# First attention: the rows of maxima go from SBUF to SBUF in three transfers, ahead of the large loads of terms

## The chip, the cores and the metric

The kernel runs on one core of one Trainium2 chip. The metric is the device time of one execution in microseconds (us); lower is better. The core's engines are TensorE (PE in the rows; its weight loads are PEld), VectorE (DVE), ScalarE (ACT), GpSimd (POOL) and SyncE (SP), which here only issues transfers. Each runs its own list of instructions in order and waits on semaphores for the others.

## The reference, cut to what matters

Two transformer layers run one after the other on 16 sequences of 256 tokens with 128 channels. The first half of the first layer, which alone is touched, is:

```python
h = _layernorm(x, axis=-1) * (1 + ca) + sa
# _L0_attn_ref, 16 heads of 8 channels
q = apply_rope(q) * scale
k = apply_rope(k)
dots = jnp.einsum('bnih,bnjh->bnij', q, k)
dots = jnp.where(mask, jnp.float32(-100000.0), dots)
attn = jax.nn.softmax(dots, axis=-1)
o = jnp.einsum('bnij,bnjh->bnih', attn, v)
return o @ Wo.T + bo
x = x + ga * _L0_attn_ref(h, ...)
```

A mixture of experts, a sparse second attention and a second mixture of experts follow.

## The kernel before

The function `attention0` handles one sequence (one batch, index k from 0 to 15) in each turn of a software pipeline. A turn mixes stages that belong to different batches: in the turn of batch k, stage C computes the scores, exponentials and outputs of batch k, D finishes the output projection of batch k-1, M and N compute the row maxima of batches k+1 and k+2 (M the second half of the groups of heads, N the first), S loads the terms of k+2, A projects, rotates and splits batch k+4, and L takes the layer norm's statistics of batch k+5. I call the turn of batch k turn k; turns -5 to -1 only fill the pipeline. The order inside a turn is written out by hand for each engine, in the `run(...)` lists at the end of each engine's block.

The scores are computed twice. Queries and keys are split into bf16 parts whose products add up to an fp32 product; the combinations ("terms", 48 rows) are written to DRAM (`a0_terms_d`) and read back into `qs` and `ks`. Each batch's terms are read back twice, 384 KB for each of `qs` and `ks` each time: by `spread_parts` into rows 64 to 111 for stages M and N (L381), and by `spread_again` into rows 0 to 47 for stage C (L394). Stages M and N compute the masked scores, and VectorE reduces each bank to the negated row maxima (`maxima`, L734). These are split into three bf16 parts, turned by TensorE (`turn_max`, L587), copied to `nparts` (48 partitions by 256) by ScalarE (`take_max`, L496), and moved into rows 48 to 50 of `qs` by `spread_max`, through DRAM (L401, then L403). Rows 48 to 50 meet ones in `ks`, so that stage C's matmul (L541) gives score minus maximum.

TensorE starts a turn with three groups of scores, which I call (0,0), (0,1) and (0,2) after the stage C part of each; every group begins with a mask matmul of stage M (L508; the one of (0,2) is the first in a turn with 512 columns). The waits that matter at a turn's start are in `open_c`: the semaphores `c_spread` (the loads of L394) and `nspread` (the row transfer of L403). Group (0,2) reuses the bank of (0,0), so it waits until VectorE has reduced that bank. After (0,2) come `outputs(3)` of the batch before (L601, L603), which waits for GpSimd's `keep(3)` (L442). Late in the turn stand the projections of stage A (L624), VectorE's rotation (L711, L713), GpSimd's sum (L422) and then the square root of the layer norm (L414, L416), and last on VectorE's list `normalise` (L700).

SP's list in a turn is `spread_again`, `spread_max`, `spread_parts`:

```python
run(sp, [("S", spread_again), ("M", spread_max), ("A", spread_parts)])
```

Of the kernel before, what the change touches and what calls it, by code (L numbers as in the profile page):

```python
# [11 lines left out]
BF16 = mybir.dt.bfloat16  # L12
# [3 lines left out]
B, L, D = 16, 256, 128  # L16
# [3 lines left out]
H, HD = 16, 8  # L20
# [228 lines left out]
def hold(eng, sem, per, b, n):  # L249


    if per * b.k + n > 0:
        eng.wait_ge(sem, b.x * per + n)


def pipeline(eng, first, last, start, end, body, turns=3):


    passes = (end - start) // turns
    for k in range(first, start):  # L260
        body(Batch(k, k))
    with eng.Fori(0, passes) as i:
        for r in range(turns):
            body(Batch(i * turns + (start + r), start + r))
    for k in range(start + passes * turns, last):
        body(Batch(k, k))


def attention0(nc, s, t, ps):
# [21 lines left out]
    TOP = ROWS  # L291
    UN = 12
    with ExitStack() as ctx:
        def sb(name, shape, dt=F32):
            return ctx.enter_context(nc.sbuf_tensor("a0_" + name, shape, dt))

        def sem(name):
            return ctx.enter_context(nc.semaphore("a0_" + name))
# [12 lines left out]
        qs = sb("qs", [M_ROW + ROWS, 3, H, L], BF16)  # L311
# [3 lines left out]
        nparts = sb("nparts", [3 * H, L], BF16)  # L315
# [5 lines left out]
        yo = sb("yo", [P, L])  # L321
        unit, pause = sb("unit", [P, 1]), sb("pause", [P, 1])
        terms_d = nc.dram_tensor("a0_terms_d", [3, 2, len(TERMS), P, L], BF16).ap()
        nparts_d = nc.dram_tensor("a0_nparts_d", [3 * H, L], BF16).ap()

        cleared = sem("cleared")
        stats_done, rstd_done, y_done = sem("stats_done"), sem("rstd_done"), sem("y_done")
# [3 lines left out]
        m_spread, c_spread = sem("m_spread"), sem("c_spread")  # L331
        m_full, m_read = sem("m_full"), sem("m_read")
        nT_full, nT_read = sem("nT_full"), sem("nT_read")
        nsplit, nstored, nspread = sem("nsplit"), sem("nstored"), sem("nspread")
        c_full, exp_done = sem("c_full"), sem("exp_done")
        kept = sem("kept")
        pv_done, o_read = sem("pv_done"), sem("o_read")
# [11 lines left out]
        def run(eng, order):  # L349

            ahead = {"D": -1, "C": 0, "M": 1, "N": 2, "S": 2, "A": 4, "L": 5}

            def body(b):
                for stage, step in order:
                    if stage == "B":
                        step(b)
                        continue
                    c = b + ahead[stage]
                    if 0 <= c.k < B:
                        step(c)  # L360
            pipeline(eng, -5, B + 1, 2, B - 5, body)

        @block.sync
        def _(sp):
            def own_rows(side, b):

                return terms_d[b.k % 3, side].rearrange("t (d h) n -> (t d) (h n)", h=H)

            def spread_parts(b):


                sp.wait_ge(split, b.x + 1)
                for n, m in RUNS:
                    sp.dma_start(terms_d[b.k % 3, 0, n:n + m].rearrange("t p n -> p t n"),
                                 parts[:, 0, TERMS[n][0]].unsqueeze(1).to_broadcast([P, m, L])).then_inc(q_stored, 16)
                for n, m in RUNS:
                    sp.dma_start(terms_d[b.k % 3, 1, n:n + m].rearrange("t p n -> p t n"), parts[:, 1, 0:m]
                                 ).then_inc(k_stored, 16)
                for dst, side, done in ((qs, 0, q_stored), (ks, 1, k_stored)):
                    sp.wait_ge(done, b.x * STORE + STORE)  # L380
                    sp.dma_start(dst[M_ROW:M_ROW + ROWS, b.k % 3].rearrange("p h n -> p (h n)"), own_rows(side, b)  # L381
                                 ).then_inc(m_spread, 16)
                if b.k == 1:
                    for name, src in (("wg", "e0_wg"), ("wu", "e0_wu"), ("wd", "e0_wd"), ("wr", "e0_wr")):
                        sp.dma_start(s["e0_w"][name][:], t[src]).then_inc(s["e0_in"], 16)
                    sp.dma_start(s["e0_w"]["bias"][:], t["L0_ffn_e_score_bias"].partition_broadcast(P)
                                 ).then_inc(s["e0_in"], 16)

            def spread_again(b):


                hold(sp, c_full, UN, b + -3, UN)
                for dst, side in ((qs, 0), (ks, 1)):
                    sp.dma_start(dst[0:ROWS, b.k % 3].rearrange("p h n -> p (h n)"), own_rows(side, b)  # L394
                                 ).then_inc(c_spread, 16)

            def spread_max(b):


                sp.wait_ge(nT_read, b.x + 1)  # L400
                sp.dma_start(nparts_d, nparts[:]).then_inc(nstored, 16)  # L401
                sp.wait_ge(nstored, b.x * 16 + 16)
                sp.dma_start(qs[TOP:TOP + 3, b.k % 3], nparts_d.rearrange("(t h) n -> t h n", h=H)).then_inc(nspread, 16)  # L403

            run(sp, [("S", spread_again), ("M", spread_max), ("A", spread_parts)])

        @block.gpsimd
        def _(pool):
# [48 lines left out]
        @block.scalar  # L457
        def _(act):
            def modulate(b):
                hold(act, a_full, A_STEPS, b, 1)  # L460
                nc.scalar.activation(hT[:, b.k % 3], ps[:, 6, 0:L], ACT.Identity, bias=sa[:], scale=ca[:]).then_inc(a_read, 1)

            def exps(g, n):
                def step(b):
                    if n == 0:
                        hold(act, pv_done, HG, b, g - 1)
                    act.wait_ge(c_full, b.x * UN + 3 * g + n + 1)
                    bank = 2 + (3 * g + n) % 2
                    if n < 2:
                        dst, src = pr[:, g % 2, 2 * n:2 * n + 2, 0:L], ps[:, bank].rearrange("p (j n) -> p j n", j=2)  # L470
                    else:
                        dst, src = pr[:, g % 2, :, L:L + P], ps[:, bank].rearrange("p (j n) -> p j n", j=HJ)
                    nc.scalar.activation(dst, src, ACT.Exp).then_inc(exp_done, 1)  # L473
                return step

            def outputs(a):
                def step(b):
                    act.wait_ge(pv_done, b.x * HG + 2 * a + 2)
                    hold(act, d_full, D_STEPS, b, -3)
                    nc.scalar.activation(o[:, 2 * a:2 * a + 2], ps[:, 4 + a].rearrange("p (g n) -> p g n", n=L),  # L480
                                         ACT.Copy).then_inc(o_read, 1)
                return step

            def turned(b):
                act.wait_ge(d_full, b.x * D_STEPS + 3)
                nc.scalar.activation(onT[:], ps[:, 7, 0:L], ACT.Copy).then_inc(d_read, 1)

            def projected(b):
                act.wait_ge(d_full, b.x * D_STEPS + 4)
                nc.scalar.activation(yo[:], ps[:, 7, 0:L], ACT.Identity, bias=ga[:, 1:2], scale=ga[:, 0:1]  # L490
                                     ).then_inc(d_read, 1)

            def take_max(b):
                act.wait_ge(nT_full, b.x + 1)
                hold(act, nspread, 16, b, 0)
                nc.scalar.activation(nparts[:], ps[0:3 * H, 6, 0:L], ACT.Copy).then_inc(nT_read, 1)  # L496

            run(act, [("C", exps(0, 0)), ("C", exps(0, 1)), ("C", exps(0, 2)), ("D", outputs(1)),
                      ("C", exps(1, 0)), ("C", exps(1, 1)), ("C", exps(1, 2)), ("A", modulate),
                      ("C", exps(2, 0)), ("D", turned), ("C", exps(2, 1)), ("M", take_max), ("C", exps(2, 2)),  # L500
                      ("C", outputs(0)), ("D", projected), ("C", exps(3, 0)), ("C", exps(3, 1)),
                      ("C", exps(3, 2))])

        @block.tensor
        def _(pe):
# [4 lines left out]
            def open_c(g, n):  # L510

                def step(b):
                    if g == 0 and n == 0:
                        pe.wait_ge(c_spread, b.x * SPREAD + SPREAD)
                        pe.wait_ge(nspread, b.x * 16 + 16)
                    hold(pe, exp_done, UN, b, 3 * g + n - 1)
                return step

# [1554 lines left out]
```

## Time and profile before

| | us |
|---|---|
| median of 3 runs | 1315.09 |
| lowest and highest of the 3 | 1312.11, 1319.2 |
| the profiled execution, its own time | 1318.88 |
| span of the profiled execution | 1317.0 |
| first attention, turns 0 to 15 | about 85 to 429 of the span |
| TensorE busy over the span | 1017.9 (77%) |
| VectorE, ScalarE, GpSimd busy | 827.5 (63%), 481.6 (37%), 386.9 (29%) |

The rows further down come from that one profiled execution. A row of the timeline gives the start, the duration, the engine, the line, and in brackets how long the engine had sat idle before it and what released it; "x2" means two instructions merged in one row. Transfers are issued by SP's queue (SPq); the duration of such a row is that of the issue, not of the transfer, for which the profile has a time "to landing".

### The profile page before, as it was taken

How to read it: one execution, taken by the hardware profiler on the slowest of the kernel's cores; microseconds unless marked ns; L12 is line 12 of the kernel's file. 1: busy time of each engine (PE TensorE's matmuls, PEld its weight loads, DVE VectorE, ACT ScalarE, POOL GpSimd, SP SyncE). 2: the span in 40 equal slices, each digit the busy share in tenths (PEclk: the TensorE clock that was granted, in tenths of full speed). 3: DMA queues.
4: the chain of work that ended last, by engine and by line, in shares of the span. 5: the costliest groups of instructions: out<-in, count | busy, mean ns of one | idle time of the engine just before them, and what ended most of it. 6: DMA issues, size and time to landing. Idle time of an engine off the chain costs nothing. (4 is left out here: it accounts for less than half of the span.)

```text
span 1317.0 us, 25195 instructions
## 1 busy us (share of the span) xinstructions
PE 1017.9 (77%) x9122; PEld 615.3 (47%) x9153; DVE 827.5 (63%) x1910; ACT 481.6 (37%) x839; POOL 386.9 (29%) x475
## 2 busy tenths in 40 slices
PE   3667878787878699999999997588988898844230
PEld 2333434343434344444444443377777777734120
DVE  4556666766651566667666654498889898566222
ACT  0024444444444233323323321465665565311110
POOL 4336454645522100000000001443333331016436
PEclk9998888888886699999999999589999999855575
DMA  4884656565620722321422230333322322040232
GB/s 120 215 153 76 133 89 130 90 124 95 128 47 2 245 81 89 106 91 66 127 91 78 92 107 23 97 99 99 87 72 91 99 71 79 1 128 33 75 110 77
DMA packets 86037, 125.69 MB, mean 95 GB/s; under 512 B 10170, under 2 KB 54128, under 8 KB 82176
## 3 DMA queue, kind: packets, MB, share of 16 engines
q1 hardware_dynamic: 83888, 120.98, 35.6%
q0 software_dynamic: 2048, 3.37, 0.9%
q8 instruction: 63, 1.03, 0.3%
q14 instruction: 38, 0.31, 0.1%
HBM read 92.50 MB, written 32.65 MB: 95 GB/s over the span
## 5 line engine op out<-in xcount | busy, mean ns | idle before, releaser
L473 ACT ACTIVATE a_pr<-ps 128x512 f32<-128x512 f32 x192 | 113.2, 597 | 161.6 <-PE ps L541 160.8
L922 ACT ACTIVATE e_sg<-ps 128x512 f32<-128x512 f32 x136 | 81.2, 597 | 245.2 <-PE ps L947 235.3
L734 DVE TENSOR_REDUCE a_nmax<-ps 128x2 f32<-128x512 f32 (+1 forms) x192 | 128.7, 686 | 55.8 <-PE ps L552 54.7
L1111 DVE TENSOR_TENSOR e_up<-e_sg,ps 128x512 f32<-128x512 f32 x128 | 87.9, 687 | 107.2 <-PE ps L954 101.3
L947 PE MATMUL ps<-e_hT,e_wg 128*128 128x512 f32 x272 | 141.3, 601 | 0.8 <-DVE e_wT L1098 0.8
L963 PE MATMUL ps<-e_hm,e_wd 128*128 128x512 f32 x272 | 139.2, 593 | 1.5 <-DVE e_pause L1109 0.8
L954 PE MATMUL ps<-e_hT,e_wu 128*128 128x512 f32 x272 | 139.8, 596 | 0.0
L508 PE MATMUL ps<-a_mask,identb 128*128 128x256 bf16 (+1 forms) x161 | 57.6, 358 | 68.3 <-DMA a_qs<-a_nparts_d 37.1
L1114 DVE TENSOR_TENSOR e_hm<-e_up,e_wb 128x512 f32<-128x512 f32 x128 | 88.5, 692 | 5.6
L541 PE MATMUL ps<-a_qs,a_ks 51*128 51x256 bf16 (+1 forms) x512 | 85.1, 276 | 6.0 <-ACT a_pr L473 1.5
L552 PE MATMUL ps<-a_ks,a_qs 48*128 48x256 bf16 (+1 forms) x512 | 87.7, 280 | 1.2 <-DVE a_nmax L734 0.7
L898 POOL TENSOR_TENSOR e_rstd<-e_mv,eps 128x4 f32<-128x4 f32 x8 | 1.6, 201 | 290.9 <-DVE e_mv L1025 290.9
L1643 POOL TENSOR_TENSOR a_prod<-a_q,a_kp 128x768 f32<-128x768 f32 (+1 forms) x32 | 53.5, 1692 | 112.1 <-PE ps L1851 108.9
L963 PEld LDWEIGHTS ps<-e_hm,e_wd 128*128 128x128 f32 x272 | 51.4, 190 | 67.5 <-issue 63.6
L954 PEld LDWEIGHTS ps<-e_hT,e_wu 128*128 128x128 f32 x272 | 52.1, 192 | 66.0 <-issue 60.3
L442 POOL TENSOR_SCALAR_AFFINE_SELECT a_pr<-a_pr 128x512 f32<-128x512 f32 x128 | 78.4, 637 | 0.1
L947 PEld LDWEIGHTS ps<-e_hT,e_wg 128*128 128x128 f32 x272 | 49.9, 192 | 53.1 <-issue 51.7
L1923 DVE TENSOR_TENSOR a_lg<-ps,a_gw 128x1024 f32<-128x1024 f32 x32 | 59.3, 1894 | 8.7 <-PE ps L1830 5.9
L508 PEld LDWEIGHTS ps<-a_mask,identb 128*128 128x128 bf16 x192 | 20.4, 106 | 92.7 <-issue 62.7
L541 PEld LDWEIGHTS ps<-a_qs,a_ks 51*128 51x128 bf16 x512 | 31.9, 101 | 52.5 <-issue 47.4
L439 POOL TENSOR_TENSOR a_pause<-a_unit 128x1 f32<-128x1 f32 x64 | 12.8, 200 | 133.9 <-ACT a_pr L473 133.9
L1633 POOL TENSOR_TENSOR a_rstd<-a_mv,eps 128x2 f32<-128x2 f32 x16 | 30.7, 1921 | 72.5 <-DVE a_mv L1907 72.5
(264 smaller groups left out, 2085.4 us busy)
## 6 DMA issues: line engine op xcount, KB each, us to landing
e_wb<-e_wT_d SPq DMA_DIRECT2D x128, 256.0 KB, 3.3
a_gw<-a_gd_d SPq DMA_DIRECT2D x16, 1024.0 KB, 4.9
a_qs<-a_terms_d SPq DMA_DIRECT2D x32, 384.0 KB, 5.4
a_ks<-a_terms_d SPq DMA_DIRECT2D x32, 384.0 KB, 7.1
a_gd_d<-a_gc SPq DMA_DIRECT2D x64, 132.0 KB, 2.4
a_terms_d<-a_parts SPq DMA_DIRECT2D x32, 192.0 KB, 2.2
a_terms_d<-a_parts SPq DMA_DIRECT2D x32, 128.0 KB, 2.1
a_terms_d<-a_parts SPq DMA_DIRECT2D x32, 64.0 KB, 1.8
```

The costliest lines, as they stand in the source:

```text
L442: k = nc.gpsimd.affine_select(own, own, [[0, HJ], [1, P]], ALU.is_ge, 0.0, base=0, channel_multiplier=-1)
L473: nc.scalar.activation(dst, src, ACT.Exp).then_inc(exp_done, 1)
L508: nc.tensor.matmul(out, identb[:], mask[:, 0:n], start=True, stop=False, skip_group_check=True)
L541: mm = nc.tensor.matmul(out, ks[0:TOP + 3, p, h, 0:P] if n < 2 else ks[0:TOP + 3, p, h, P:L], qs[0:TOP + 3, p, h, :] if n < 2 else qs[0:TO ...
L552: mm = nc.tensor.matmul(out, qs[M_ROW:M_ROW + ROWS, p, h, P:L] if n < 2 else qs[M_ROW:M_ROW + ROWS, p, h, 0:P], ks[M_ROW:M_ROW + ROWS, p, ...
L734: nc.vector.tensor_reduce(dst, src, AX_X, ALU.max, negate=True).then_inc(m_read, 1)
L922: nc.scalar.activation(sg[:, par], ps[:, 2 + par], ACT.Silu).then_inc(silu_done, 1)
L947: nc.tensor.matmul(ps[:, 2 + par, :], wg[:, u, :], hT[:, b.k % 2, :], start=True, stop=True).then_inc(gates_full, 1)
L954: nc.tensor.matmul(ps[:, 4 + par, :], wu[:, u, :], hT[:, b.k % 2, :], start=True, stop=True).then_inc(ups_full, 1)
L963: nc.tensor.matmul(ps[:, 0, :], wd[:, u, :], hm[:, (b.k + u) % 2, :], start=(u == 0), stop=(u == UNITS - 1), skip_group_check=True).then_i ...
L1111: nc.vector.tensor_tensor(up[:, par], sg[:, par], ps[:, 4 + par], ALU.mult).then_inc(up_done, 1)
L1114: nc.vector.tensor_tensor(hm[:, par], up[:, par], wb[:, (u - 1) % RING], ALU.mult).then_inc(hidden_done, 1)
```

## The change

The buffer in DRAM is dropped. `spread_max` issues three transfers, one for each of the three parts, that each read 16 partitions of `nparts` (512 bytes in each) and write one partition of `qs` (8 KB). The semaphore `nspread` therefore counts 48 for a batch where it counted 16, and SP waits for no transfer between them. On SP's list `spread_max` now stands ahead of `spread_again`.

```diff
         terms_d = nc.dram_tensor("a0_terms_d", [3, 2, len(TERMS), P, L], BF16).ap()
-        nparts_d = nc.dram_tensor("a0_nparts_d", [3 * H, L], BF16).ap()
...
-        nsplit, nstored, nspread = sem("nsplit"), sem("nstored"), sem("nspread")
+        nsplit, nspread = sem("nsplit"), sem("nspread")
...
                 sp.wait_ge(nT_read, b.x + 1)
-                sp.dma_start(nparts_d, nparts[:]).then_inc(nstored, 16)
-                sp.wait_ge(nstored, b.x * 16 + 16)
-                sp.dma_start(qs[TOP:TOP + 3, b.k % 3], nparts_d.rearrange("(t h) n -> t h n", h=H)).then_inc(nspread, 16)
-
-            run(sp, [("S", spread_again), ("M", spread_max), ("A", spread_parts)])
+                for t in range(3):
+                    sp.dma_start(qs[TOP + t:TOP + t + 1, b.k % 3], nparts[H * t:H * t + H]).then_inc(nspread, 16)
+
+            run(sp, [("M", spread_max), ("S", spread_again), ("A", spread_parts)])
...
-                hold(act, nspread, 16, b, 0)
+                hold(act, nspread, 48, b, 0)
...
-                        pe.wait_ge(nspread, b.x * 16 + 16)
+                        pe.wait_ge(nspread, b.x * 48 + 48)
```

Only SP's instructions move; the other engines keep their order. The first place is SP's queue where the pipeline fills, between the end of turn -2 and the start of turn 0. `a_terms_d` is the buffer of terms in DRAM and `a_nparts_d` the dropped one. Before:

```order
L381 DMA a_qs<-a_terms_d 48x4096 [waits a0_q_stored]
L381 DMA a_ks<-a_terms_d 48x4096 [waits a0_k_stored]
L394 DMA a_qs<-a_terms_d 48x4096
L394 DMA a_ks<-a_terms_d 48x4096
L401 DMA a_nparts_d<-a_nparts 48x256 [waits a0_nT_read]
L403 DMA a_qs<-a_nparts_d 3x4096 [waits a0_nstored]
L374 DMA a_terms_d<-a_parts 128x3x256 [waits a0_split]
```

The same place in the changed kernel, where every line number up to here is smaller by one:

```order
L380 DMA a_qs<-a_terms_d 48x4096 [waits a0_q_stored]
L380 DMA a_ks<-a_terms_d 48x4096 [waits a0_k_stored]
L401 DMA a_qs<-a_nparts 1x16x256 [waits a0_nT_read]
L401 DMA a_qs<-a_nparts 1x16x256 x2
L393 DMA a_qs<-a_terms_d 48x4096
L393 DMA a_ks<-a_terms_d 48x4096
L373 DMA a_terms_d<-a_parts 128x3x256 [waits a0_split]
```

The two large loads of L394 (now L393) were ahead of the row transfer and are now behind it, and the wait on the store to DRAM is gone.

The second place is a turn in the middle of the stage, where the loads also wait for stage C of an earlier batch (`a0_c_full`). Before:

```order
L394 DMA a_qs<-a_terms_d 48x4096 [waits a0_c_full]
L394 DMA a_ks<-a_terms_d 48x4096
L401 DMA a_nparts_d<-a_nparts 48x256 [waits a0_nT_read]
L403 DMA a_qs<-a_nparts_d 3x4096 [waits a0_nstored]
L374 DMA a_terms_d<-a_parts 128x3x256 [waits a0_split]
```

In the changed kernel:

```order
L401 DMA a_qs<-a_nparts 1x16x256 [waits a0_nT_read]
L401 DMA a_qs<-a_nparts 1x16x256 x2
L393 DMA a_qs<-a_terms_d 48x4096 [waits a0_c_full]
L393 DMA a_ks<-a_terms_d 48x4096
L373 DMA a_terms_d<-a_parts 128x3x256 [waits a0_split]
```

The loads now stand behind the wait for `nT_read`, which ScalarE gives in the middle of the turn.

## Rows read from the trace of the kernel before

**Rows 1.** Turn 4, busy us: PE, PEld, DVE, ACT, POOL; clock; DMA; GB/s.

```profile
171.00:193.00 22.00, 17.87 (x168) 9.53 (x170) 15.41 (x37) 9.76 (x18) 11.33 (x19) 0.84 0.60 111
```

**Rows 2.** Waits of TensorE from 45 to 420: us in total, times, longest.

```profile
PE ps L508 <- DMA a_qs<-a_nparts_d: 37.1, 11, 9.2
PE ps L508 <- DVE a_nmax L734: 21.2, 27, 3.8
PE ps L508 <- issue: 9.5, 3, 6.1
```

**Rows 3.** Timeline of SP's queue in turn 4: start, duration, queue, line.

```profile
180.61 0.34 SPq L394 DMA_DIRECT2D a_qs<-a_terms_d  x1
...
185.10 0.30 SPq L401 DMA_DIRECT2D a_nparts_d<-a_nparts  x1
191.51 0.24 SPq L403 DMA_DIRECT2D a_qs<-a_nparts_d  x1
```

**Rows 4.** Timeline, end of turn 4 and start of turn 5, by engine.

```profile
188.17 1.13 PE L624 MATMUL ps<-a_hT,a_w 128*128 128x256 f32 x4
...
189.74 0.47 DVE L713 SCALAR_TENSOR_TENSOR a_rb<-ps,a_bcol,a_sink 128x256 f32<-128x256 f32 x1
...
190.30 1.27 POOL L422 TENSOR_TENSOR a_ra<-a_ra,a_rb 128x512 f32<-128x512 f32 x1 [2.83 <-DVE a_rb L713]
...
193.80 2.29 DVE L700 TENSOR_SCALAR a_y<-x,a_mv,a_rstd 128x128 f32 x2 [1.03 <-POOL a_rstd L416]
...
193.94 0.39 PE L508 MATMUL ps<-a_mask,identb 128*128 128x256 bf16 x1 [2.49 <-DMA a_qs<-a_nparts_d]
...
196.02 1.27 DVE L734 TENSOR_REDUCE a_nmax<-ps 128x2 f32<-128x512 f32 x2
...
196.75 0.61 PE L508 MATMUL ps<-a_mask,identb 128*128 128x512 bf16 x1 [1.01 <-DVE a_nmax L734]
```

**Rows 5.** Timeline of TensorE at the start of turn 1.

```profile
102.63 0.27 PE L508 MATMUL ps<-a_mask,identb 128*128 128x256 bf16 x1 [0.54 <-DVE a_nmax L734]
...
107.66 0.59 PE L508 MATMUL ps<-a_mask,identb 128*128 128x512 bf16 x1 [3.84 <-DVE a_nmax L734]
```

**Rows 6.** Timeline while the pipeline fills, up to turn 0, by engine.

```profile
68.17 0.38 ACT L496 ACTIVATE a_nparts<-ps 48x256 bf16<-48x256 f32 x1 [2.47 <-PE ps L587]
...
72.59 0.32 SPq L381 DMA_DIRECT2D a_ks<-a_terms_d  x1
...
79.00 2.29 DVE L700 TENSOR_SCALAR a_y<-x,a_mv,a_rstd 128x128 f32<-128x128 f32 x2 [1.53 <-POOL a_rstd L416]
...
85.62 0.37 PE L508 MATMUL ps<-a_mask,identb 128*128 128x256 bf16 x1 [9.21 <-DMA a_qs<-a_nparts_d]
...
86.60 0.69 DVE L734 TENSOR_REDUCE a_nmax<-ps 128x2 f32<-128x512 f32 x1 [5.31 <-PE ps L552]
```

**Rows 7.** Landing times of L401; issues (first and last start) and landing of L381.

```profile
DMA to landing us min/median/max: 1.4/6.8/9.6
...
L381 SPq DMA_DIRECT2D a_ks<-a_terms_d x16: 303/318/318, 36.4 to 356.8; - x16
...
DMA to landing us min/median/max: 4.5/5.6/7.2
```

**Rows 8.** Timeline, starts of turns 12 and 13, with `keep(3)` and L401.

```profile
349.34 0.27 PE L508 MATMUL ps<-a_mask,identb 128*128 128x256 bf16 x1 [2.96 <-issue]
...
350.13 1.23 POOL L442 TENSOR_SCALAR_AFFINE_SELECT a_pr<-a_pr 128x512 f32<-128x512 f32 x2
...
360.43 0.30 SPq L401 DMA_DIRECT2D a_nparts_d<-a_nparts  x1
...
371.02 0.37 PE L508 MATMUL ps<-a_mask,identb 128*128 128x256 bf16 x1 [6.13 <-issue]
```

**Rows 9.** Timeline of TensorE, group (0,2) of turns 6 and 7.

```profile
218.53 0.61 PE L508 MATMUL ps<-a_mask,identb 128*128 128x512 bf16 x1 [1.64 <-DVE a_nmax L734]
...
241.20 0.61 PE L508 MATMUL ps<-a_mask,identb 128*128 128x512 bf16 x1 [0.92 <-DVE a_nmax L734]
```

## The prediction

> **What bounds the kernel now.** I read four views, in this order. First the busy times of a steady turn, for the limit: in 22 us TensorE is busy 17.87, VectorE 15.41, GpSimd 11.33, and TensorE's granted clock averages 0.84 [rows 1]. No engine fills the turn, so a loop of waits sets it. Second, TensorE's waits over the stage: 37.1 us in 11 waits for the row transfer, 21.2 us in 27 for VectorE's maxima, and 9.5 us in 3 that the view names "issue" [rows 2]. The three are the starts of turns 12, 13 (2.96 and 6.13 [rows 8]) and 14 (what is left of 9.5: 0.4), where TensorE resumes about two us after L403, so they are the same wait. Together 46.6 us hang on this transfer, and it is tempting to take that as the gain.
>
> Third, SP's queue, for why the transfer is late. In turn 4 the rows are ready and the store is issued at 185.10, but SP issues the next step at 191.51, once the store has landed: 6.4 us for 24 KB [rows 3]. The same store landed in 1.4 us at best and 9.6 at worst [rows 7]. The large loads issued from 180.61 on are ahead of it in the same queue. The way back adds 193.94 - 191.51 = 2.43 us.
>
> Fourth, the timeline across a turn's boundary, which decides [rows 4]. TensorE is held until 193.94, does (0,0) and (0,1), and then waits again, 1.01 us, at (0,2) until 196.75. That wait is for VectorE's reduction of bank (0,0), which began at 196.02, right behind `normalise` (193.80 plus 2.29). `normalise` waited for GpSimd, which began its sum at 190.30, released by VectorE's rotation of 189.74, which followed TensorE's projection (188.17 plus 1.13). None of this waits for the row transfer. The loop that closes a turn is: (0,2), TensorE's work up to the projection, rotation, GpSimd's sum and root, `normalise`, reduction, next (0,2).
>
> **The steady turns, 1 to 11.** If the rows arrive early, TensorE starts turn 5 at 193.94 - 2.49 = 191.45 and has (0,0) and (0,1) done some 1.5 us later. VectorE runs its list in order and reaches (0,0) at 196.02 all the same, and (0,2) starts at 196.75 all the same. The trace holds this case already: in turn 1 TensorE was not held by the transfer (it began at 102.63, released by VectorE), and then waited 3.84 us at (0,2), until 107.66 [rows 5]. L = 5 batches ahead, so `normalise` runs to the end of turn 10, and it gates (0,2) of turns 1 to 11. Ten of the 11 waits for the transfer fall into these turns: 37.1 - 9.21 = 27.9 us that move to VectorE. Gain: 0.
>
> **Turn 0.** TensorE is idle 9.21 us before 85.62. The rows had been ready since 68.55 (68.17 plus 0.38), while SP stood at the loads of L381 until 72.59 plus 0.32 [rows 6]. In the changed order the three transfers are issued next, 72.95 to about 74.2 at 0.24 to 0.42 us an issue. Ahead of them in the queue are only the L381 loads, which take 4.5 to 7.2 us to land [rows 7], so they are through at 77.1 to 79.8, and the rows land in between or just behind: I take 79, and 80.5 as late. VectorE is busy with `normalise` until 79.00 + 2.29 = 81.29 and reduces (0,0) then, instead of at 86.60. TensorE needs 1 us for (0,0), so up to a landing at 80.3 the gain is 86.60 - 81.29 = 5.3 us; at 80.5 it is 5.1. The rest of the 9.21 goes to VectorE's wait.
>
> **Turn 12.** No `normalise` precedes it, so TensorE starts 2.96 us earlier. Behind (0,2) it needs `keep(3)`, which GpSimd ends at 350.13 + 1.23 = 351.36 [rows 8]; today TensorE, with some 2.5 us of groups (my estimate), comes to it at about 351.8. Gain: 0.4.
>
> **Turn 13.** The rows are ready by the issue at 360.43; TensorE is free at 371.02 - 6.13 = 364.89 [rows 8]. The L381 loads of the last batch, issued up to 356.8, are the only large ones ahead now (the L394 loads, issued just behind them today, go behind the rows), and they land within 7.2 us [rows 7], by 364.0. Gain: 6.1. Turn 14 gives its 0.4.
>
> **TensorE's clock.** After the idle 6.13 us the mask matmul of turn 13 takes 0.37 us, against 0.27 at turn 12 [rows 8]: the lower level (1.2 GHz) against the higher (2.4). Without the gap turn 13 should run its first part at the higher level. Some 5 us of matmuls at about 0.3 less is an estimate of 1.5 us.
>
> **What moves on SP.** The loads of L394 for batch k+2 leave about 5.5 us later (186.1 instead of 180.61). Those sent in turn 4 are for turn 6, whose (0,2) is at 218.53 [rows 9], so it starts about 3 us before; even twice the longest landing of L381, 14.4 us, has them there by 201. SP's wait for `nT_read` ends at 185.1, and `spread_parts` waits for GpSimd's split, whose first step starts only at 190.30: nothing is blocked behind it. Three issues replace two, under 0.5 us more on a queue with slack. Cost: 0, with some 14 us of cover.
>
> **The new transfer's price.** The trace has no SBUF to SBUF transfer. Below it is bounded by 1.4 us, above by 9.6 [rows 7]. In the steady turns, where the queue ahead is nearly drained at 185.1, I take 2.5. Its bound of harm: (0,0) must start by about 195.1, so a landing up to 10 us after issue costs nothing.
>
> By the Trainium skill (DMA: Bandwidth & Descriptors, Rules for kernel authors) small transfers should be joined, since below 64 KB one pays mostly overhead; three of 8 KB in place of one of 24 KB go against it. This trace puts the fastest 24 KB store at 1.4 us, and by either reading the extra overhead falls inside the slack just worked out.
>
> **Sum.** 5.3 + 0 + 0.4 + 6.1 + 0.4 + 1.5 = 13.7 us. The profiled execution took 1318.88, 3.8 above the median of 1315.09, so it would become 1305.2, and the median 1301.4. I say 1301; its own range is 1296 to 1306. 0.5% (6.6 us) is about what a measurement of this kernel can tell from no change.
>
> **Rivals.**
> - The whole wait goes, 46.6 us, to 1268.5. For it: the totals of rows 2. Against: rows 4 and 5. It needs `normalise` to finish earlier, and nothing in the change does that. 0.03.
> - The clock eats part. The two idle pieces of a turn (2.49 and 1.01) become one of about 4. In the trace two lengths of turn alternate: (0,2) to (0,2) is 21.78 us for turn 5 [rows 4, 9] and 22.67 for turn 6 [rows 9], with the same work. If all 11 turns became long, 5 to 6 of them lose 0.9, about 5 us: 1306. For it: idle time moves against whatever decides the clock. Against: turn 1 has the merged gap already. If all became short, 1296. 0.12 for the long case. The Trainium skill (TensorE: Matmul & The Clock Gate, Why this matters for your kernels) warns of a long idle gap between bursts of matmuls, since it lowers the clock; that speaks for this rival.
> - The ends stay hidden: the three transfers land late behind the L381 loads in turns 0 and 13, beyond 85 and 370. Then about 1 us is left, 1314. Against: 72.95 to 85 is 12 us where the row maximum is 9.6. 0.05.
> - Slower: 16 partitions gathered into one, three times, take over 10 us from issue to landing in every turn. It decides from 10 us on, in turns 1 to 11; at 13 us it costs 3 x 11 = 33 less the 13.7, about 1334. Against: the 24 KB of L403 went into three partitions and were there in 2.43 us. 0.03.
> - My forecast: 0.77.
>
> **The numbers.** Faster by over 0.5% (below 1308.5): forecast nearly whole, 0.75, first rival 0.03, most of the clock's, 0.08: 0.86. Within 0.5%: 0.11. Slower: 0.03. The range 1293 to 1309 takes in the short and long clock cases and leaves out the rivals at 1268, 1314 and 1334 with a margin for the median of three.
>
> **What the changed profile would show.** TensorE's wait for the row transfer near nothing, its wait for VectorE at L508 up from 21.2 to about 50 us with some 4 us at each (0,2) of turns 1 to 11; the distance between these as before, 22.2 as the mean of 21.78 and 22.67; turn 0's (0,2) about 5 us earlier; turn 13 right behind turn 12; attention over some 14 us earlier. I am wrong if the turns' distance falls (the loop is not closed as I say), if it rises (clock, or a late transfer, which its landing time would tell apart), or if a wait on `c_spread` appears.

## The result and the profile after

| | before | changed |
|---|---|---|
| median, us | 1314.65 (5 runs) | 1299.51 (5 runs) |
| lowest to highest | 1312.11 to 1319.2 | 1297.93 to 1308.03 |
| span of the profiled execution | 1317.0 | 1306.1 |
| first attention ends (SP issues the next stage's first load) | 428.98 | 412.60 |

The ratio is 0.9891, with a 95% interval of 0.9856 to 0.9925: the change makes the kernel about 15 us faster (10 to 19 by the interval), where 13.7 had been forecast. The profiled execution of the changed kernel was its slowest, 1308.03, so the two spans above differ by only 10.9 us.

The changed kernel's waits of TensorE from 45 to 420 (us in total, times, longest), against [rows 2]:

```profile
PE ps L506 <- DVE a_nmax L732: 50.4, 44, 3.8
...
PE ps L506 <- DMA a_qs<-a_terms_d: 4.9, 4, 3.4
```

The wait for the row transfer, 37.1 us before, has no row of its own any more, and the wait for VectorE's maxima has gone from 21.2 to 50.4. So of 46.6 us of waiting on a transfer, 29.2 came back under another engine's name. (The 4.9 us are named after the large loads. The largest of the four, 3.4 us at turn 0, is the wait for the rows: two more profiles of the same kernel put it down to `a_qs<-a_nparts`, 3.2 and 3.5 us. The other three, about 0.5 us each, I do not count so, for the reason that turn 5 shows below.)

The start of turn 5, timeline rows of SP's queue, TensorE, VectorE and GpSimd, in order of time, against [rows 4]:

```profile
181.48 1.78 SPq L401 DMA_DIRECT2D a_qs<-a_nparts  x3
...
187.57 0.66 DVE L732 TENSOR_REDUCE a_nmax<-ps 128x2 f32<-128x512 f32 x1
...
188.29 0.28 PE L506 MATMUL ps<-a_mask,identb 128*128 128x256 bf16 x1 [0.45 <-DMA a_qs<-a_terms_d]
...
190.18 2.29 DVE L698 TENSOR_SCALAR a_y<-x,a_mv,a_rstd 128x128 f32 x2 [1.02 <-POOL a_rstd L414]
192.39 1.28 DVE L732 TENSOR_REDUCE a_nmax<-ps 128x2 f32<-128x512 f32 x2
...
192.48 1.23 POOL L440 TENSOR_SCALAR_AFFINE_SELECT a_pr<-a_pr 128x512 f32<-128x512 f32 x2
...
193.13 0.39 PE L506 MATMUL ps<-a_mask,identb 128*128 128x512 bf16 x1 [3.31 <-DVE a_nmax L732]
```

TensorE starts the turn with hardly a wait (0.45 us instead of 2.49), and then stands 3.31 us at group (0,2), for a reduction that VectorE begins the moment `normalise` ends. That is the picture of turn 1 before [rows 5], now in every turn from 1 to 11. The 0.45 us are not a wait for the rows: their issues end at 183.26, and with the 1.9 us that such a transfer takes in the median to land they are there by about 185.2, 3 us before TensorE goes on. What ends at that moment is VectorE's reduction of 187.57 (plus 0.66 is 188.23).

Turn 0, timeline of SP's queue, TensorE and VectorE, against [rows 6]:

```profile
73.04 1.91 SPq L401 DMA_DIRECT2D a_qs<-a_nparts  x3
...
79.88 0.37 PE L506 MATMUL ps<-a_mask,identb 128*128 128x256 bf16 x1 [3.38 <-DMA a_qs<-a_terms_d]
...
81.30 1.28 DVE L732 TENSOR_REDUCE a_nmax<-ps 128x2 f32<-128x512 f32 x2
```

The reduction of bank (0,0) moved from 86.60 to 81.30, and it now starts when `normalise` lets it. The rows are there for TensorE at 79.88, where 79 was forecast and 80.3 was the latest that costs nothing: a margin of 0.4 us.

Turns 12 and 13, timeline of TensorE, against [rows 8]:

```profile
343.97 0.38 PE L506 MATMUL ps<-a_mask,identb 128*128 128x512 bf16 x1 [0.37 <-DVE a_nmax L732]
347.54 1.10 PE L599 MATMUL ps<-a_pr,a_vv 128*32 128x256 f32 x8 [2.87 <-POOL a_pr L440]
...
364.72 0.38 PE L506 MATMUL ps<-a_mask,identb 128*128 128x512 bf16 x1 [0.36 <-DVE a_nmax L732]
```

Group (0,2) of turn 12 is early, but `outputs(3)` (L599) then waits 2.87 us for GpSimd's `keep(3)`. The 6.13 us gap before turn 13 is gone.

The starts of (0,2) in all profiles taken of both kernels, from their timelines, give the gain by stretch (us; two profiles before, three of the changed kernel):

| stretch | before | changed | gain, mean |
|---|---|---|---|
| up to (0,2) of turn 0 | 87.44, 88.48 | 82.12, 82.39, 82.01 | 5.8 |
| turn 0 to turn 11 | 242.62, 244.41 | 244.21, 241.76, 244.78 | -0.1 |
| turn 11 to turn 13 | 42.77, 43.21 | 38.39, 37.18, 35.98 | 5.8 |
| turn 13 to turn 14 | 16.77, 16.54 | 14.01, 14.02, 14.02 | 2.6 |
| turn 14 to the stage's end | 39.38, 33.31 | 33.87, 33.86, 32.89 | 2.8 |
| the second attention | 322.1, 324.4 | 327.7, 327.2, 325.2 | -3.4 |

The first four rows, 14.1 us, are the stretches that the forecast names. The 0.1 in the second row is uncertain by 1 to 2 us, since single profiles of one kernel differ there by up to 3 us. The last two rows are taken up under the clock.

### The profile page after: what moved, and what is told of

Same layout as the page of the kernel before. It is cut to its first block and busy times, and to the rows that moved or that the text cites. A ratio compares the mean times of both kernels' runs of the same rounds, so it can differ in the third digit from the quotient of the medians.

```text
span 1306.1 us, 25202 instructions
## 1 busy us (share of the span) xinstructions
PE 1021.6 (78%) x9122; PEld 624.9 (48%) x9153; DVE 827.4 (63%) x1910; ACT 481.6 (37%) x839; POOL 390.3 (30%) x475
## 3 DMA queue, kind: packets, MB, share of 16 engines
q8 instruction: 63, 1.03, 0.4%
## 5 line engine op out<-in xcount | busy, mean ns | idle before, releaser
L506 PE MATMUL ps<-a_mask,identb 128*128 128x256 bf16 (+1 forms) x161 | 56.1, 349 | 55.8 <-DVE a_nmax L732 50.4
L1641 POOL TENSOR_TENSOR a_prod<-a_q,a_kp 128x768 f32<-128x768 f32 (+1 forms) x32 | 57.9, 1832 | 117.0 <-PE ps L1849 113.8
L539 PE MATMUL ps<-a_qs,a_ks 51*128 51x256 bf16 (+1 forms) x512 | 81.4, 266 | 6.1 <-ACT a_pr L471 1.5
L599 PE MATMUL ps<-a_pr,a_vv 128*32 128x256 f32 x512 | 49.0, 450 | 4.2 <-POOL a_pr L440 4.2
```

What stands on the lines that cost most here:

```text
L506: nc.tensor.matmul(out, identb[:], mask[:, 0:n], start=True, stop=False, skip_group_check=True)
L539: mm = nc.tensor.matmul(out, ks[0:TOP + 3, p, h, 0:P] if n < 2 else ks[0:TOP + 3, p, h, P:L], qs[0:TOP + 3, p, h, :] if n < 2 else qs[0:TO ...
```

## The experiments

**The changed kernel again**, for a second profiled execution.

> The changed kernel once more, for a second profiled execution. My theory: the gain inside the first attention repeats, (0,2) of turn 0 about 5.3 us and the stage's end about 16 us earlier than before. What this sample tells apart is the 5.5 us that the second attention, whose code is the same, took longer in the first profiled execution (327.7 against 322.1 us). If that was chance of the clock's phase, the second attention takes another time here (322 to 325) and the span comes to about 1300; if the change causes it, it takes 327 to 328 again.

Median 1301.71, ratio 0.9882 (0.9852 to 0.9912), span 1302.4. (0,2) of turn 0 came at 82.39 and the stage ended at 409.21, which repeats the gain. The second attention took 327.2 us, which by what I had written spoke for the change as the cause. A third profile of it (below) took 325.2.

**The order alone.**

```diff
-            run(sp, [("S", spread_again), ("M", spread_max), ("A", spread_parts)])
+            run(sp, [("M", spread_max), ("S", spread_again), ("A", spread_parts)])
```

> The order alone: the rows still go through DRAM in two transfers, but ahead of the large loads. My theory: the store lands in about 2 us instead of 6.4 in a steady turn, the rows are there by 190 where 191.4 is needed, so steady turns are as in the changed kernel. Turn 0: store behind the first loads until about 79, rows at 81.5, 1 us later than VectorE is free, so (0,2) some 4 us earlier than before. Turn 13: 1 to 2 us later than in the changed kernel. In sum 11 to 14 us faster than before, 1301 to 1304. Rival (the saved round trip through DRAM is what counts): 3 us or less, 1311 or more.

Median 1300.38, ratio 0.9877 (0.9854 to 0.9901): as much as the changed kernel's 0.9882, with the rows still going through DRAM. Time from issue to landing of the store in this kernel:

```profile
DMA to landing us min/median/max: 1.4/1.8/6.0
```

The median fell from 6.8 us [rows 7] to 1.8, because nothing large is ahead. (0,2) of turn 0 is at 82.94, 0.8 later than in the first profile of the changed kernel, about as forecast.

**The route alone.** The changed kernel with the two entries swapped back.

```diff
-            run(sp, [("M", spread_max), ("S", spread_again), ("A", spread_parts)])
+            run(sp, [("S", spread_again), ("M", spread_max), ("A", spread_parts)])
```

> The route alone: three transfers within SBUF, but behind the large loads as before. My theory: the rows land about 6.5 us after issue in steady turns, which is about when TensorE is free, so nothing changes there; turn 0 starts at about 82 and gains 3 to 4 us; turn 13 waits for rows behind the loads until about 367 and gains 3; in sum 6 to 9 us, 1306 to 1309. If the order is worthless and the route everything, the gain is the changed kernel's, 15 us.

Median 1309.84, ratio 0.9947 (0.9923 to 0.997): 4.8 us by the medians and 7 by the ratio, where I had said 6 to 9, and 9.5 us slower than the order alone. The sum is near, its first term is not: (0,2) of turn 0 is at 86.97, about 1 us earlier than before and not 3 to 4, because the rows landed behind all four large loads only at 85.15 and not at 82. Landing times of the three transfers, and group (0,2) of turn 5:

```profile
DMA to landing us min/median/max: 1.8/6.0/9.9
```

```profile
195.67 0.39 PE L506 MATMUL ps<-a_mask,identb 128*128 128x512 bf16 x1 [2.79 <-DVE a_nmax L732]
```

Behind the loads the rows take 6.0 us, about what the store took before. In this steady turn that costs nothing: (0,2) waits for VectorE all the same.

**Normalise moved away.** The changed kernel with VectorE's `normalise` moved from the end of a turn to behind the second reduction of the next (there the same batch is stage A's, hence the letter).

```diff
-            run(v, [("M", maxima(2, 0)), ("M", maxima(2, 1)), ("M", maxima(2, 2)), ("S", values),
+            run(v, [("M", maxima(2, 0)), ("M", maxima(2, 1)), ("A", normalise), ("M", maxima(2, 2)), ("S", values),
...
-                    ("N", maxima(1, 2)), ("L", normalise)])
+                    ("N", maxima(1, 2))])
```

> The changed kernel with VectorE's normalise moved from the end of a turn to the next turn, behind the second reduction of stage M. My theory: (0,2) no longer waits for it and comes 3 us earlier in turns 1 to 11, but then outputs(3) waits for GpSimd's keep(3), which ends only half a us before TensorE takes it up today. So the 3.5 us wait at (0,2) turns into one of 2 to 3 us at outputs(3), and the distance of turns falls by 0.5 to 1: 1290 to 1300. Rival (normalise alone closes the loop): the turns shorten by 3 us and more, 1265 or below.

Median 1298.44, ratio 0.9877 (0.9847 to 0.9908), no better than the changed kernel. From the start of `outputs(3)` in turn 1 to that in turn 11 a turn takes 22.1 us (103.25 to 323.88), against 22.1 to 22.2 in the three profiles of the changed kernel; I had said 0.5 to 1 us less. Its waits of TensorE from 45 to 420:

```profile
PE ps L599 <- POOL a_pr L440: 39.5, 13, 3.4
PE ps L506 <- DVE a_nmax L732: 11.0, 34, 0.8
```

The wait for the maxima fell from 50.4 to 11.0, and 39.5 us in 13 waits stand now at `outputs(3)`, for `keep(3)`. The same time has changed its name a second time.

**keep(3) moved alone.**

```diff
-            run(pool, [("C", keep(0)), ("C", keep(1)), ("C", keep(2)), ("A", split_parts), ("L", rstd_of),
-                       ("A", split_rest), ("C", keep(3)), ("A", last_part)])
+            run(pool, [("C", keep(0)), ("C", keep(1)), ("C", keep(2)), ("A", split_parts), ("C", keep(3)),
+                       ("L", rstd_of), ("A", split_rest), ("A", last_part)])
```

> The changed kernel with keep(3) moved alone. My theory: rstd_of now stands behind keep(3) on GpSimd, so the root of the layer norm, normalise and with them (0,2) come about 1.5 us later in turns 1 to 11, and the kernel gets 10 to 17 us slower than the changed one: 1310 to 1317. In turn 12 keep(3) no longer holds outputs(3), which gives 2 us back. Rival (keep(3), not normalise, closes the loop in the changed kernel): faster, 1290 or less.

Median 1321.34, ratio 1.0033 (1.0011 to 1.0056), slower than even the kernel before, and by the ratios about 20 us slower than the changed kernel, where I had said 10 to 17. TensorE's wait for the maxima:

```profile
PE ps L506 <- DVE a_nmax L732: 66.2, 47, 5.2
```

(0,2) goes from 103.51 in turn 1 to 342.76 in turn 11, 23.93 us a turn, against 22.21 in the first profile of the changed kernel: 1.7 us a turn longer. GpSimd computes the layer norm's root later by one `keep`: VectorE stands idle 2.36 us in the median before `normalise`, where it stood 1.03, so 1.3 of the 1.7 us are that delay; the other 0.4 I have not traced. This shows that the chain root, `normalise`, reduction sets the steady turn.

**Both moved.** The two diffs above together.

> The changed kernel with both of the other things at a turn's start moved away: normalise one turn later on VectorE (as in e3_norm) and GpSimd's keep(3) ahead of rstd_of and split_rest. My theory: in e3_norm TensorE waits 39.5 us in 13 waits for keep(3) and nothing else new, so this one opens the loop. keep(3) then ends about 3 us earlier, and turns 1 to 11 shorten by 2.5 to 3.5 us each: 1262 to 1273. Rival (something else closes the loop next to keep(3), such as GpSimd's own chain of split_parts to last_part): under 1 us a turn, 1288 or more.

Median 1280.92, ratio 0.9731 (0.97 to 0.9762), about 20 us below the changed kernel: the loop is open, but less than I said (1262 to 1273). VectorE around `normalise` in this kernel:

```profile
180.51 2.19 DVE L698 TENSOR_SCALAR a_y<-x,a_mv,a_rstd 128x128 f32 x2 [1.03 <-POOL a_rstd L414]
182.61 0.68 DVE L732 TENSOR_REDUCE a_nmax<-ps 128x4 f32<-128x512 f32 x1
```

The third reduction stands behind `normalise`, which still waits for GpSimd. I had moved it out of the way of two reductions only.

**The kernel before with both moved**, rows through DRAM and behind the loads.

> The kernel before, rows through DRAM and behind the large loads, with the same two moves as e5_both. It shows what the change is worth once nothing hides the wait. My theory: TensorE waits about 3 us for the rows at every turn's start as before; the loop then is row maxima, store, load, next turn, about 21.8 us, so the moves give 5 us at most: 1308 to 1314, and e5_both is 40 us or more faster than this one. Rival (the row transfer does not matter even then): within 10 us of e5_both.

Median 1316.22, ratio 0.9994 (0.9966 to 1.0021): no gain, where I had said 1308 to 1314. TensorE's largest wait:

```profile
PE ps L508 <- DMA a_qs<-a_nparts_d: 48.2, 9, 12.6
```

Here the row transfer is the bound. So with the loop open the change is worth 35 us (1316.22 against 1280.92), where it was worth 15 with the loop closed; I had said 40 or more.

**Normalise one step later.** Built on the kernel with both moved.

```diff
-            run(v, [("M", maxima(2, 0)), ("M", maxima(2, 1)), ("A", normalise), ("M", maxima(2, 2)), ("S", values),
+            run(v, [("M", maxima(2, 0)), ("M", maxima(2, 1)), ("M", maxima(2, 2)), ("A", normalise), ("S", values),
```

> As e5_both, with normalise one step later still on VectorE's list: behind the third reduction of stage M instead of ahead of it. e5_both came to 1280.9 where I had said 1262 to 1273, and TensorE waited there 1.3 us in a turn for the third reduction, which stood behind normalise. My theory: that wait goes and each of turns 1 to 11 shortens by about 1 us: 1267 to 1273. Rival (GpSimd's keep(3), which TensorE reaches within half a us, takes the whole wait over): within 3 us of e5_both.

Median 1277.39, ratio 0.9697 (0.9667 to 0.9728): the fastest median here, but only 3.5 us below the kernel with both moved, measured beside other runs of the kernel before, and the intervals of the two ratios overlap: a gain of this step is not shown. I had said about 10, and the rival that I named (`keep(3)` takes the wait over) within 3 us. TensorE's waits:

```profile
PE ps L599 <- POOL a_pr L440: 14.5, 16, 1.3
PE ps L613 <- DVE a_vv L719: 13.5, 13, 5.0
```

`keep(3)` and `turn_tokens` (L613, which needs `normalise` and the bank that `values`, L719, frees) took over, beside 10.6 us for VectorE's maxima. No single one is the bound any more. My price for the third reduction was wrong by the same mistake that a reader of [rows 2] would make: I counted a wait as a gain without asking who is late next.

**The same through DRAM, ahead of the loads.**

```diff
-            run(sp, [("S", spread_again), ("M", spread_max), ("A", spread_parts)])
+            run(sp, [("M", spread_max), ("S", spread_again), ("A", spread_parts)])
```

These are the moves of the kernel just above (`normalise` behind the third reduction, `keep(3)` earlier), with this line, on top of the kernel before.

> e7_later with the rows through DRAM, but ahead of the large loads as in e1_order. It tells order and route apart with the loop open. The rows are ready about 6.5 us before the next turn and the way through DRAM takes about 2 plus 2.4 us with the queue free. My theory: in steady turns they are still just in time, so it is within 4 us of e7_later, the difference coming from turn 0 and the last turns. Rival (the way through DRAM is the next wait): TensorE waits 1 us or more for the rows in each turn and the kernel is over 10 us slower than e7_later.

Median 1281.63, ratio 0.972 (0.9683 to 0.9758), 4.2 us above the last kernel, about the 4 us that I had allowed, with a ratio inside that one's interval. TensorE's wait for the rows:

```profile
PE ps L508 <- DMA a_qs<-a_nparts_d: 16.9, 6, 8.8
```

In the last kernel it was one wait of 6.3 us, at turn 0. Here it is 8.8 us at turn 0 and 0.7 to 3.0 us in five of the steady turns, and the store lands in 4.0 us in the median, not in 1.8 as with the order alone. So with the loop open the slower route is felt, but its cost, 4.2 us by the medians, is not clear of noise; to be ahead of the loads counts for more.

**Two more profiles**, of the kernel before and of the changed one.

> The kernel before once more, one look for a second profile. The second attention took 322.1 us in its first profile, 327.7 and 327.2 in the two of the changed kernel, 324.0, 325.0 and 321.0 in the experiments. If its time belongs to each kernel's phase, it is within 0.5 us of 322.1 again; if it is chance in each execution, it may be anywhere in 321 to 328.

> The changed kernel, one look for a third profile. Its second attention took 327.7 and 327.2 us in the first two, the kernel before 322.1 and 324.4, and the five experiments 321.0 to 325.0. If the change lengthens that stage, 327 us or more again; if it is chance in each execution, 325 or less is likely. From turn 14's (0,2) to the end of the first attention it should be either about 33.8 or about 39 us, as in all the others.

The second attention took 324.4 us in the first and 325.2 in the second. With the experiments its time was 320.0 to 327.7 us over thirteen profiles with the same code. It moves by 2.3 us (before) and 2.5 us (changed) between executions of one kernel, so much of it is chance; the three of the changed kernel average 3.4 above the two of before, and with two and three samples I leave it open whether the change has a part in it. The end of the first attention, from (0,2) of turn 14, took 33.3 us in the first of the two and 32.9 in the second, for which I had expected 33.8 or 39.

## Why the prediction was right

**Steady turns, gain 0.** Right, and shown from three sides. Over the eleven stretches from turn 0 to turn 11 the mean differs by 0.1 us. Making the root of the layer norm 1.3 us later lengthened the turn by 1.7 us; taking `normalise` away moved the wait to `keep(3)`, which I had named only for turn 12 but which is close behind in every turn: in turn 5 it ends at 193.71 (192.48 plus 1.23) and TensorE takes it up at 193.88, in turn 6 at 215.27 and 215.78. The rival in which the whole 46.6 us go, 28 of them in these turns, is refuted.

**Turn 0, 5.3 us.** Measured 5.8 as the mean of the profiles, 5.3 in the first pair. The bound, `normalise`, was the one named.

**Turns 12 and 13, 0.4 and 6.1 us.** Together 5.8 measured against 6.5. The split holds too: from (0,2) of turn 11 to the start of turn 12's `outputs(3)` the mean gain is 0.3 us, since the 3 us won at (0,2) are lost again to `keep(3)`, as forecast. Against the mean before, the three profiles gained 4.6, 5.8 and 7.0 us over both turns, and in the smallest of them the lower clock level lasted longest: from that `outputs(3)` to (0,2) of turn 13 it averaged 0.71 in the first profile of the changed kernel, 0.88 and 0.89 in the other two.

**Turn 14 and the clock, 0.4 and 1.5 us.** The stretch from turn 13 to 14 gave 2.6. Its granted clock was 0.84 and 0.85 in the two profiles before and 1.00 in all three of the changed kernel. The terms were right in kind and somewhat small.

**What moves on SP, cost 0.** Right: no wait of TensorE for the large loads is left that something else does not explain (the 3.4 us of turn 0 are for the rows, turn 5's 0.45 for VectorE), and the kernel with the order alone is as fast as the changed one. But the issue was under-priced. Three issues take 1.91 us at turn 0 and 1.78 in a steady turn, not the 0.24 to 0.42 each that I had from other shapes; against the two issues before (0.30 and 0.24) that is 1.2 us more, where I had said under 0.5.

**The new transfer, 2.5 us.** Its landing in the changed kernel:

```profile
DMA to landing us min/median/max: 1.8/1.9/5.7
```

With its issue, that is about 3.7 us (1.78 plus 1.9) from the first issue to the last landing in a steady turn, far inside the 10 us that it had. The slower rival is refuted. The Trainium skill's rule against small transfers (DMA: Bandwidth & Descriptors, Rules for kernel authors) speaks against three transfers. The trace agrees in that 24 KB hold the queue for 1.78 us; a turn with slack hides it. No run moves the rows within SBUF in one transfer, so what the splitting itself costs is open.

**The clock as a rival.** Steady turns did not all become long: the sum over them did not change, and the granted clock from (0,2) of turn 1 to that of turn 11 did not fall with the merged gap (0.85 in both profiles before, 0.87 to 0.88 in the changed kernel). But the clock has a say that I had not priced. From (0,2) of turn 14 the stage needs 32.9 to 34.1 us in ten of the thirteen profiles and 38.5 to 39.4 in three, and the kernel before has done both: 39.38 us at a mean granted clock of 0.66, and 33.31 at 0.89. Two windows of 5 us of the kernel before, in its first profile and in its second (columns as in [rows 1]):

```profile
405.00:410.00 5.00, 5.00 (x32) 2.73 (x32) 1.04 (x6) 1.46 (x3) 1.37 (x3) 0.50 0.01 3
```

```profile
405.00:410.00 5.00, 4.33 (x54) 2.64 (x54) 0.77 (x5) 3.44 (x7) 2.07 (x6) 1.00 0.02 3
```

At the lower level TensorE gets 32 matmuls through, at the higher 54. In the first pair of profiles this stretch gave the changed kernel 5.5 us, and the second attention took 5.5 back. How much of the 5.5 is chance is open: all three long ones are among the five profiles of kernels that send the rows through DRAM, none among the eight that do not. The forecast names neither stretch; in the means they are 2.8 us won and 3.4 lost. That a sum of 13.7 met 15.1, itself known only to within some 5 us, is therefore partly luck.

## What to carry to other kernels

Before counting a wait as a gain, follow the next wait of the same engine and ask whether its releaser depends on the first; if it does not, as here, only the turns without that second wait gain (here the first and the last few). Put a small, urgent transfer ahead of large ones that are not urgent; that alone gave the whole gain, and the shorter route added nothing on top that could be measured (alone, behind the large transfers, it gave a third to a half of it). Where two chains end within half a us of each other, move both: here each move alone gave nothing or a loss, both together 20 us.

## What the runs showed of the hardware

An issue of the SBUF to SBUF transfer, 16 partitions of 512 bytes into one, holds SP's queue 0.59 us in the median (0.51 at least), against 0.24 for the 24 KB from DRAM into three partitions and 0.30 for the store of 48 partitions. Its landing of 1.8 to 1.9 us with the queue free is no shorter than that of the store to DRAM, 1.4 us at best and 1.8 in the median of the order alone, though the shapes differ: leaving out DRAM saved a second transfer here, not latency in one. And the same code took 33.31 or 39.38 us in one stretch of two executions, at a mean granted clock of 0.89 or 0.66.
